# Two sweeps over the experts, with the token choice spread over the output stage and the first sweep

## The reference

```python
x = layernorm(x + attention(x))    # 16 causal heads of 64; keys and values from a latent of 128
# experts, per batch of 1024 tokens
scores = softmax(x @ router_w.T)                        # 8 experts
gate_vals, sel_idx = top_k(scores transposed, 257)      # every expert chooses 257 tokens of each batch
tokens = x[b_idx, sel_idx]
h = gelu(tokens @ w1[e] + b1[e])                        # 256 -> 1024
y = h @ w2[e] + b2[e]                                   # 1024 -> 256
out = zeros.at[b_idx, sel_idx].add(y * gate_vals)
x = layernorm(x + out)
```

## Time and profile before

| | us |
|---|---|
| median of 3 runs (lowest, highest) | 3337.62 (3337.56, 3338.99) |
| the profiled execution | 3334.53 |
| its span, first to last instruction | 3332.8 |

### The profile page before, as it was taken

One profiled execution on the slowest core, in us unless ns is written; L12 is line 12 of the kernel. 1 busy time (PEld: TensorE's weight loads), 2 busy tenths in 40 slices (PEclk: granted clock), 3 DMA queues, 4 the chain that ended last, 5 costly groups with the idle time before them and its releaser, 6 DMA issues. The chain is left out here.

```text
span 3332.8 us, 62849 instructions
## 1 busy us (share of the span) xinstructions
PE 3114.2 (93%) x20414; PEld 2500.8 (75%) x20414; DVE 2093.2 (63%) x5850; ACT 1875.5 (56%) x4071; POOL 1376.6 (41%) x1543
## 2 busy tenths in 40 slices
PE   7999999999999999999999999889808999999995
PEld 5777776777777777777777777589808999999995
DVE  4666666666666666666666666566584555555555
ACT  5766666667666666667666667543203434333335
POOL 3433333433343333334343334312214655545555
PEclk9999999999999999999999999999959999999997
DMA  4444444444444444445444444277502333323337
GB/s 106 108 115 105 101 121 96 108 119 100 104 119 99 107 109 107 109 107 121 97 110 118 100 106 106 57 280 265 183 14 62 74 74 71 78 36 66 75 57 212
DMA packets 179818, 358.55 MB, mean 108 GB/s; under 512 B 23488, under 2 KB 107840, under 8 KB 177472
## 3 DMA queue, kind: packets, MB, share of 16 engines
q1 hardware_dynamic: 149824, 304.33, 35.3%
q0 software_dynamic: 29696, 50.48, 7.5%
HBM read 111.39 MB, written 75.56 MB: 56 GB/s over the span
## 5 line engine op out<-in xcount | busy, mean ns | idle before, releaser
L189 POOL TENSOR_SCALAR prob<-prob,inv 128x128 f32<-128x128 f32 (+7 forms) x1024 | 774.1, 756 | 1296.7 <-DVE inv L579 1289.6
L574 DVE CUSTOM_DVE_ANT_0 s_ps<-s_ps,mask 128x128 f32<-128x128 f32 (+7 forms) x1024 | 781.4, 763 | 673.3 <-PE s_ps L308 655.6
L476 ACT ACTIVATE prob<-s_ps,neg_max 128x128 f32<-128x128 f32 (+7 forms) x1024 | 760.5, 743 | 346.3 <-DVE neg_max L574 329.6
L307 PE MATMUL s_ps<-k_hh,q_hl 128*128 128x512 f32 (+3 forms) x1536 | 588.7, 384 | 32.7 <-ACT prob L476 21.8
L323 PE MATMUL t_ps<-ident,prob 128*128 128x128 f32 x4096 | 611.1, 274 | 1.2 <-DVE prob_t L640 0.5
L339 PE MATMUL o_ps<-prob_t,v 128*64 128x512 f32 (+3 forms) x3072 | 537.5, 492 | 1.5 <-DVE y L596 1.5
L557 ACT ACTIVATE prob_t<-t_ps 128x512 f32<-128x512 f32 (+3 forms) x704 | 377.2, 536 | 282.1 <-PE t_ps L323 275.6
L323 PEld LDWEIGHTS t_ps<-ident,prob 128*128 128x128 f32 x4096 | 474.9, 140 | 52.0 <-issue 5.1
L308 PE MATMUL s_ps<-k_lz,q_hl 128*128 128x512 f32 (+3 forms) x1536 | 512.9, 346 | 0.0
L307 PEld LDWEIGHTS s_ps<-k_hh,q_hl 128*128 128x128 f32 x1536 | 289.2, 188 | 180.3 <-ACT prob L476 73.7
L339 PEld LDWEIGHTS o_ps<-prob_t,v 128*64 128x64 f32 x3072 | 204.0, 136 | 286.4 <-issue 267.6
(11 more groups left out here) (189 smaller groups left out, 5550.3 us busy)
## 6 DMA issues: line engine op xcount, KB each, us to landing
k_hh<-k_high SPq DMA_DIRECT2D x256, 256.0 KB, 4.1
q_hl<-q_high SPq DMA_DIRECT2D x128, 256.0 KB, 4.0
q_hl<-q_low SPq DMA_DIRECT2D x128, 256.0 KB, 4.3
k_lz<-k_low SPq DMA_DIRECT2D x128, 256.0 KB, 5.1
y_d<-y SPq DMA_DIRECT2D x128, 256.0 KB, 3.8
c_yt<-y_d SPq DMA_DIRECT2D x16, 2048.0 KB, 8.2
w_raw<-w SPq DMA_DIRECT2D x16, 1024.0 KB
b_xt<-x_t SPq DMA_DIRECT2D x8, 1024.0 KB, 7.7
```

What stands on the lines that cost most here:

```text
L189: pool.tensor_scalar(pr, pr, inv[:, s % 4:s % 4 + 1], 1.0, ALU.mult, ALU.mult).then_inc(norm_done, 1)
L307: pe.matmul(out, q_hl[u][h][:, cols], k_hh[u][h][:, w], start=True, stop=False)
L476: act.activation(prob[s % 4][:, 0:(q + 1) * P], s_ps[s % 2][:, 0:(q + 1) * P], ACT.Exp, scale=-1.0, bias=neg_max[:, s % 4:s % 4 + 1], accu ...
L574: dve.tensor_tensor_reduce(part, part, mask[:, T - (q + 1) * P:T], 1.0, -MASKED, ALU.add, ALU.min, neg_max[:, s % 4:s % 4 + 1]).then_inc(m ...
```

## The change

The change has four parts.

- **Attention to output.** A class `Bridge` holds buffers that outlive attention. In the last batch SP loads w_out into the buffer of x; ACT and DVE split it in the last pair (slots 0, 2, 4, 6). Ahead of the last pair's stores SP loads y of group 0 into the buffers of q and k.
- **Output stage.** No loop. POOL makes three of four low parts of y from group 2 on, ACT normalises (with a shift that POOL makes), SP issues the stores of x1 behind its loads. After group 6 the score of batches 0 to 2 is turned, and DVE takes four rounds of the top-k in each of groups 7 to 14 and the last in group 15, half before and half after the probabilities. At the end the lists of batches 0 to 2 are merged, and the score of all batches is kept. w1 of expert 0 is loaded in this stage.
- **Choosing.** The stage is gone. The lists of all batches come from 33 rounds in units 0 to 10 of the expert stage, three in each: two before the bias additions, one between them. They are turned in unit 11 and merged in unit 12.
- **Experts.** No loop, and two sweeps. Sweep 1 (n = 0 to 7) runs each expert over the six tiles of batches 0 to 2, in two units of 384. Sweep 2 (n = 8 to 15) runs each expert over the ten tiles of batches 3 to 7 and the short tile of all batches: units of 512, 512 and 264, and for the last expert 264 and four of 256. All weights are loaded and split twice, thus at 15 changes of expert. In sweep 2, experts n = 8 to 13 each close one of the six groups of batches 0 to 2 (measured in step 1, closed in step 2). Their 24 tokens of the short tile that get their share later are gathered, normalised and scattered into the output again near the end (`fix_...`).

The core of the diff:

```diff
+NA = 3
...
+def best_eight(dve, K, n):
+    new = slice(8 * n, 8 * n + 8)
+    if n:
+        dve.wait_ge(K.gone, n)
+    dve.max(K.vals[:, new], K.score[:]).then_inc(K.maxed, 1)
+    dve.wait_ge(K.maxed, n + 1)
+    dve.max_index(K.places[:, new], K.vals[:, new], K.score[:]).then_inc(K.found, 1)
+    dve.wait_ge(K.found, n + 1)
+    dve.match_replace(K.score[:], K.vals[:, new], K.score[:], -1.0).then_inc(K.gone, 1)
...
+            for m in range(NPAIR):
+                if m == NPAIR - 1:
+                    sp.wait_ge(scores_done, 16 * (NPAIRS - 1))
+                    sp.wait_ge(y_out[0], 16 * NPAIR + 1)
+                    for c, part in enumerate(R.yt):
+                        sp.dma_start(part, y_d[0][:, 2 * c:2 * c + 2, :]).then_inc(R.yt_in, 16)
...
+            for n in range(G):
+                rounds = range(STARTS[n], STARTS[n + 1] if n + 1 < G else ROUNDS)
+                early = len(rounds) // 2
+                measure(n)
+                if n:
+                    logits(n - 1)
+                if n + 2 < G:
+                    low(n + 2)
...
+                for r in rounds[:early]:
+                    best_eight(dve, K, r)
+                if n:
+                    probabilities(n - 1)
+                for r in rounds[early:]:
+                    best_eight(dve, K, r)
...
+    early, late, short = full(*range(NA)), full(*range(NA, B)), (None, None)
+    for n in range(NE):
+        add(n, early[:NA])
+        add(n, early[NA:])
+    for n in range(NE, 2 * NE - 1):
+        add(n, late[:4])
+        add(n, late[4:8])
+        add(n, late[8:] + [short])
+    for b in range(NA, B):
+        add(2 * NE - 1, full(b) + [short] * (b == NA))
...
+        def quarters(x):
+            if x.n == NV - 1:
+                return []
+            return [[0, 1], [2, 3]][step_of(x)] if len(units_of(x.n)) == 2 else [[0, 1], [2], [3]][step_of(x)]
...
+            for x in UNITS:
+                if x.i + 2 <= LAST:
+                    pool.wait_ge(turned, 2 * x.i + 2)
+                    gather(UNITS[x.i + 2])
+                for c in quarters(x):
+                    weights_low(x.n + 1, c)
+                for k in ended(x.i - 2):
+                    spread(k)
+                scatter(x)
+                for k in early_group(x, 1):
+                    spread(k)
...
+            def hidden(x):
+                N, u = x.width(), x.n % 2
+                if step_of(x) == 0:
+                    if x.n == 0:
+                        pe.wait_ge(w_low_first, 2)
+                    else:
+                        pe.wait_ge(w_low, 4 * x.n + 2)
+                pe.wait_ge(t_low, 2 * x.i + 2)
...
+            for x in UNITS:
+                hidden(x)
+                if x.i < LAST:
+                    turn(UNITS[x.i + 1])
+                outputs(x)
...
+                if x.i < LAST:
+                    tokens_high(UNITS[x.i + 1])
...
+                gated(x)
...
+                for k in early_group(x, 2) + ended(x.i - 2):
+                    close(k)
+                for c in quarters(x):
+                    if step_of(x) == 0:
+                        act.wait_ge(g_done, x.before + 1)
+                    weights_high(x.n + 1, c)
...
+                rounds = range(min(ROUNDS, PER * x.i), min(ROUNDS, PER * x.i + PER))
+                for r in rounds[:2]:
+                    best_eight(dve, K, r)
+                for k in early_group(x, 1) + ended(x.i - 2):
+                    measure(k)
...
+                for q in range(count):
+                    if q == 2:
+                        for r in rounds[2:]:
+                            best_eight(dve, K, r)
```

More of the change, by code:

```diff
@@ L1 @@
 from contextlib import ExitStack
+from dataclasses import dataclass
 import numpy as np
@@ L539, in slots @@
                         exp(n, s + 2)
+                    if not after and s in WO_SPLIT:
+                        wo_high(WO_SPLIT.index(s))
                     if (m, s) in X_SPLIT and not last_batch(n):
@@ L670, in output_stage @@
     NQ = NPAIR // MQ
+    SCORE_AT = 2 * NA
+    ROUNDS_AT = [0 if n <= SCORE_AT else 4 for n in range(G)]
+    STARTS = [min(ROUNDS, sum(ROUNDS_AT[:n])) for n in range(G)] + [ROUNDS]
     with ExitStack() as ctx:
@@ new lines, in load_first, with rows, width, batches @@
+def load_first(sp, L, w1, e):
+    sp.dma_start(L.w1_raw.rearrange("p (k h) -> p k h", h=HID), w1[e].rearrange("(k p) h -> p k h", p=P)
+                 ).then_inc(L.w1_in, 16)
+@dataclass
+class Unit:
+    i: int
+    n: int
+    tiles: list
+    before: int
+    def rows(self, q):
+        return B if self.tiles[q][0] is None else P
+    def width(self):
+        return sum(self.rows(q) for q in range(len(self.tiles)))
+    def batches(self):
+        return {c for b, _ in self.tiles for c in (range(B) if b is None else (b,))}
@@ new lines, in all_units, with add @@
+def all_units():
+    units = []
+    def add(n, tiles):
+        units.append(Unit(len(units), n, tiles, sum(len(x.tiles) for x in units)))
+    full = lambda *bs: [(b, f) for b in bs for f in range(FULL)]
+    early, late, short = full(*range(NA)), full(*range(NA, B)), (None, None)
[8 more added lines that the diff above has]
+        add(2 * NE - 1, full(b) + [short] * (b == NA))
+    return units
@@ L1405, in outputs @@
+                        pe.matmul(out, hid_hi[:, m, cols], w2_lo[u][:, w], start=False, stop=False)
+                        mm = pe.matmul(out, hid_lo[:, m, cols], w2_hi[u][:, w], start=False, stop=(m == HC - 1))
                     mm.then_inc(y_done, 1)
-            def unit(n, u, g, last):
-                hidden(n, u, g)
-                ahead = later(n, u, g, 1, last)
-                if ahead:
-                    turn(*ahead)
-                outputs(n, u, g)
-            pe.wait_ge(const_ready, 2)
@@ L1466, in close, with gated @@
-            def close(i):
-                v = i % FB
-                act.wait_ge(f_shift, i + 1)
+            def gated(x):
+                for q in range(len(x.tiles)):
+                    rows = x.rows(q)
+                    act.wait_ge(b_done, x.before + q + 2)
+                    if q == 0 and x.i >= 2:
+                        landed(act, x.i - 2)
+                    act.activation(yg[x.i % 2][0:rows, q, :], yb[0:rows, q, :], ACT.Copy, scale=gates_of(x, q)
+                                   ).then_inc(g_done, 1)
```

1203 lines of the change are left out of this document (630 added, 573 removed).

## The result

The changed kernel takes 3459.6 us (median of 4 runs, 3457.7 to 3461.4) against 3338.3 of the kernel before beside it: a ratio of 1.036, interval 1.035 to 1.038. The forecast was slower, 3414 us, with a range of 3350 to 3460. So the sign is right and the size 46 us too low; the time lies 0.4 us inside the upper end of the range. One of six executions of the kernel with the lows apart took 3853.5 us in a slower state of the core, at a granted clock of 0.747, and is left out of that kernel's time. The profiled execution has a span of 3458.1, 125.3 more than before.

The account below looks back on a forecast made before the run. PE was taken as the bound, busy 93% of the span, with about 130 us open at two seams. Terms sum to +76.6 on 3332.8, so 3409.4; adding 1.7 around the span and 3.1 to the median gives 3414 us, range 3350 to 3460.

Parts of the forecast that it names:

- seam 1: Between attention and output stage: w_out and y prepared in attention's last pair let PE start earlier, -14.5 us.
- output stage: Groups with top-k rounds need 14.4 us of DVE against PE's 13.7: +5 us, bounds 0 and 20.
- seam 2: From last c_z to first e_h: most of the choosing leaves this path, 112.4 us becoming 31.8, -80.6.
- experts and end: Expert stage and what follows: boundary waits, quarter lag and clock, less the loop's gap and last-expert gains, +166.7 us.
- the clock term: After each of 15 waits at changes of expert, the granted clock halves for about 4 us: +28.5 us.
- the rival with DVE as the bound: Sweep 1: rounds or casts held longer, lag reaches step-0 units, output stage takes 20: +50 on top, 3460 us; chance 0.14.
- The boundary waits: At 15 changes of expert PE waits for all four weight quarters: +70.7 us in sweep 1, +52 in sweep 2.
- The lag behind the quarters: In expert units, w_lo on POOL holds DVE's CASTs, delaying hid_lo and PE: +26 us, bounds 0 and 50.
- The last expert and the loop's gap: Expert stage: the loop's gap goes, -6.5 us; the last expert's narrower units close fewer groups at once, -4.
- The rule that the prediction took for hid_lo: VectorE instructions with two SBUF inputs are held by GpSimd ones; without it the lag term is about 4 us smaller.

Follow-up runs that it names:

- the kernel with the lows apart: On the kernel with stores one group later and split weight wait (3303.9 us), sweep 1's second w_lo moved behind POOL's scatters: 3315.2 us.
- stores later: From the changed kernel, SP issues the x1 stores of group n-3 instead of n-2 ahead of the next y load: 3418.8 us.
- on ACT: From the changed kernel, ACT instead of SP issues the x1 stores, behind its own copies of the normalised group: 3417.8 us.
- split-wait run: From the changed kernel, PE's hidden waits only for weight quarters 0 and 1, outputs for 2 and 3: 3346.7 us.
- the quarters first: From the changed kernel, in sweep 2 ACT makes the last quarter's high part before closing the earlier group's tiles: 3462.1 us.
- the gathers behind: From the changed kernel, ACT makes weight quarters before closes, and POOL makes the weights' low parts before its gathers: 3555.2 us.
- the last two runs: Against stores later plus split wait (3303.9 us), sweep 1's second w_lo moved behind POOL's scatters: 3315.2 us; or behind its gathers, beside DVE's rounds: 3289.8 us.

## Why the prediction was right in sign and short by 46 us

The forecast by its own terms, against the two spans:

| term | forecast | measured | from |
|---|---|---|---|
| seam 1 | -14.5 | -14.6 | windows, attention's 0.9 included |
| output stage | +5 | +51.6 | windows |
| seam 2 | -80.6 | -77.2 | windows |
| experts and end | +166.7 | +165.5 | 172.9 - 7.4 |
| sum | +76.6 | +125.3 | |

**The step that failed** is the output stage, and in it one sentence: "The stores of x1 go to SP's queue, which has nothing else to do in that time than load." It prices the stores by SP's free time. What they cost is their place: a store in a queue that is served in order waits for the normalisation, and the loads behind it wait too. I added up PE, DVE and POOL group by group and never followed load, split, normalisation and store around once. Nor did I cost a clock there: 33.0 of the 51.6 are PE's idle time, 18.7 its longer busy time at the lower granted clock, and the clock term counted the changes of expert alone. The runs with the stores later or on ACT take 42.5 and 44.8 of the stage's 51.6 away. What remains, 9.1 and 6.8, is the term that I did price: 15.0 us in groups with rounds, 14.1 without, where I had 14.4 and 13.7, for +5. The lower bound of 0 and the upper of 20 were both for DVE and didn't cover a serial loop. That the time still lies within the range is luck: its upper end of 3460 came from the rival with DVE as the bound.

**Seam 1** is right: first c_z at 2164.74, 14.6 earlier than in the earlier trace rows. The block changes, put at 1 and 0.8 us, show in no row by themselves. **Seam 2** is right within 3.4; the tokens of the first gathers come 11.2 us after PE's last work.

**The boundary waits** are right in place, number, releaser and cause (the chain of row and split-wait run), and 110.9 instead of 122.7: 8.45 in the five changes with rounds (forecast 9.8), 7.0 in the sixth (7.5) and 6.7 in the next two (7.1); in sweep 2 9.0, 7.5 and four of 6.8 (7.9 each), and 4.4 in the last (4.6). I had placed sweep 1's last yb some 1.4 too late, and the end of POOL's gathers 1 too late; that these end the wait in sweep 2 is shown by the runs with the quarters first and with the gathers behind.

**The clock** was costed at 28.5. The first hidden of each expert, from its first e_h to its end, exceeds the same width without a wait ahead by 1.2 to 2.9, 30.0 over 15.

**The lag behind the quarters** was costed at 26 (23 and 3). In the list of waits it looks like 4.7 us, and I first read it as nearly absent. The e_y chains measured from start to end tell: 10.9 against 8.9 in five of sweep 1's second units and 10.2 to 11.5 in the other three, 15.2 in that sweep, and some 10 in sweep 2 (12.85 against 11.76 in the second 512 unit, and 9.0 to 9.3 against 8.9 in the short one, seven times each). So about 25, less in sweep 1 and more in sweep 2. That w_lo beside CASTs causes it in sweep 1 is shown by the last two runs, which make it larger and smaller; for sweep 2 it is argued only. By the Trainium skill (SBUF — State Buffer, Who interferes with whom) a CAST can be held by a GpSimd instruction, and a VectorE instruction with at most one SBUF input outside the two-port modes isn't; here the CAST took 3.37 beside a w_lo while the round's instruction kept 0.69 and yb its length, so the trace agrees. The rule that the prediction took for hid_lo, with two inputs in SBUF, shows as well: with the lows apart one takes 4.03 beside a w_lo, where the others take 0.55.

```profile
2499.03 4.03 DVE L1665 TENSOR_TENSOR hid_lo<-raw,hid_hi 128x384 fp32r<-128x384 f32 x1
...
2499.74 2.90 POOL L1443 TENSOR_TENSOR w_lo<-b_xt,w_hi 128x1024 fp32r<-128x1024 f32 x1
```

**The last expert and the loop's gap** were -10.5. The gap is gone. In the kernel before, the last expert's 256-wide hidden already met a wait for raw and took 13.67 us instead of the 5.6 of the other experts. In the changed kernel two such units meet one of 2.88 each, behind eight closes of 4.03 us on ACT, and hidden takes 11.4 and 9.05 instead of 5.9. So 8.6 us stand in place of 8.0, and the gain is the 7.4 behind the last e_h: some 7 where I had 4.

```profile
3291.99 0.58 PE L1387 MATMUL e_h<-tok_hi,w_hi 128*128 128x256 f32 x1 [6.04 <-ACT raw L1451]
```

**That the experts' sum is within 1.2** is partly luck. Summed over all units, the waits ahead of a hidden are 11.8 below the forecast and the end gains 3.4 more; against that the e_y chains are 33.1 longer than before (427.2 against 394.1, of which some 25 are the lag and the rest are chains that are longer without any) where I had 26, hidden is 31.1 longer (408.6 against 377.5) where I had 28.5 less the loop's 2, and what lies between takes 2.4 more, where I had nothing.

The rival "DVE is the bound of sweep 1" ends at 3460 too, by number alone: in the changed kernel its lag didn't reach the first units, and the output stage was held by SP's order, not by DVE.

## What to carry to other kernels

A DMA that waits has no cost of its own, and still costs what stands behind it in its queue. When stores and loads move into one queue, follow a single group around (load, split, normalise, store, next load), and put each store behind the loads that don't need it. When two loops share engines, cutting one shows the next: look at the pace of groups with and without the second loop's work, not at the total.

A wait for all parts of a double-buffered operand should be split by first use, before one tries to make the parts faster: here that gave back 113 of the 121 us by which the changed kernel was slower. And moving work ahead on an in-order engine moves everything else behind what that work waits for; ask who waits for what is passed.

A consumer that follows its producer piece by piece shows as busy. Measure the length of its chain against the same chain elsewhere, not its idle time.

## What the runs showed of the hardware that was not expected

A CAST of 128x384 whose record starts 0.24 us ahead of that of a w_lo on POOL still took 3.37 instead of 0.35 (in the run with the lows apart); the starts on POOL are rough (this w_lo is 2.91 long, others 2.4), so which of the two began first stays open. The top-k's instructions on DVE kept 0.69 beside a w_lo of 2.44.

The clock behind short waits, in rows of windows. The changed kernel, behind the two idle stretches of 2.88 us in the last expert, then the kernel with the split wait, behind an idle stretch of 0.97:

```profile
3408.40:3412.60 4.20, 4.17 (x19) 4.17 (x20) 3.25 (x11) 2.01 (x5) 1.31 (x2) 0.50 0.39 63
3426.10:3429.30 3.20, 3.10 (x26) 3.11 (x27) 3.06 (x12) 2.56 (x7) 1.14 (x3) 1.00 0.41 47
```

```profile
2600.00:2602.00 2.00, 2.00 (x13) 2.00 (x12) 2.00 (x2) 0.82 (x2) 2.00 (x2) 1.00 0.00 0
```

So the stretch of 0.97 cost no clock behind it. Of the two of 2.88, the first cost 5.5 us, 2.9 of idle and 2.6 behind it, and the second 3.15, at full clock behind it. The length of a wait alone doesn't tell here whether the clock falls.
